# Value products two rows at a time, and a block's own position bias as a factor applied by GpSimd

## What is computed

```python
scores = jnp.einsum('bhid,bhjd->bhij', q, k) / scale
scores = scores + _alibi_bias(N_HEADS, seq_len, M_SLOPE, x.dtype)[None]   # -|i - j| * 0.5 ** head
attn = jax.nn.softmax(scores, axis=-1)
out = jnp.einsum('bhij,bhjd->bhid', attn, v)
```

## Time and profile before

| | |
|---|---|
| median of 3 runs | 598.14 us (596.93 to 600.79) |
| profiled execution, its own time | 600.86 us |
| its span | 598.4 us |
| TensorE busy | 530.7 us, 89% |
| VectorE busy | 406.8 us, 68% |
| ScalarE busy | 339.9 us, 57% |
| GpSimd busy | 217.9 us, 36% |
| mean granted TensorE clock | 0.945 |

### The profile page before, as it was taken

The page is one execution under the profiler, slowest core; times in us unless marked ns, Lnnn a source line. Parts: engine busy times, 40 slices in busy tenths (PEclk is TensorE's granted clock), DMA queues, the critical chain, the costliest instruction groups (busy, mean ns, idle before and its releaser), DMA issues.

```text
span 598.4 us, 11849 instructions
## 1 busy us (share of the span) xinstructions
PE 530.7 (89%) x4499; PEld 298.6 (50%) x4499; DVE 406.8 (68%) x699; ACT 339.9 (57%) x665; POOL 217.9 (36%) x404
## 2 busy tenths in 40 slices
PE   6579999999999999999999999899999389999910
PEld 4234444444445454543445555555656247888710
DVE  2597877878797758789875769988695862232217
ACT  4245766767676767766777667667776013232405
POOL 5736452311234315102640520254012753554540
PEclk9797999999999999999999999999999569999965
DMA  7622343322322222221213333110000114353124
GB/s 162 172 83 76 70 122 87 96 90 77 114 87 73 91 77 100 86 82 48 69 52 70 82 87 104 29 42 21 28 12 19 58 43 109 103 142 81 54 90 133
DMA packets 49991, 48.22 MB, mean 81 GB/s; under 512 B 13923, under 2 KB 39381, under 8 KB 49936
## 3 DMA queue, kind: packets, MB, share of 16 engines
q1 hardware_dynamic: 41600, 32.26, 19.7%
q0 software_dynamic: 5488, 12.73, 6.9%
q10 hardware_dynamic: 2848, 2.49, 1.3%
HBM read 32.00 MB, written 16.06 MB: 80 GB/s over the span
## 4 chain that ended last, share of the span: by engine, by line
PE 72%; DVE 15%; DMA 5%; POOL 3%; issue 2%; ACT 1%; another core or an unknown queue 1%; POOLq 0%; ACTq 0%; DVEq 0%; SPq 0%
PE ps L958 33%; PE ps L1020 17%; DVE row_max L1486 8%; PE ps L1205 6%; PE ps L1219 5%; PE ps L960 4%; POOL xd L845 2%; DMA max_dram<-max_turned 2%; PE ps L1060 1%; DVE x_tok L1796 1%; DMA k_stacks<-k_late 1%; DVE heads L1557 1%; DMA q_stacks<-max_dram 1%; DMA w_nat<-in_qkv_w 1%
## 5 line engine op out<-in xcount | busy, mean ns | idle before, releaser
L1486 DVE TENSOR_REDUCE row_max<-ps 128x1 f32<-128x1024 f32 x256 | 297.1, 1211 | 90.6 <-PE ps L958 47.5
L1323 ACT ACTIVATE probs<-ps 128x512 f32<-128x512 f32 x512 | 268.3, 606 | 89.5 <-PE ps L960 47.8
L958 PE MATMUL ps<-k_stacks,q_stacks 96*128 96x512 bf16 x448 | 145.5, 390 | 13.7 <-DMA k_stacks<-k_late 6.1
L958 PE MATMUL ps<-q_stacks,k_stacks 99*128 99x512 bf16 (+1 forms) x512 | 142.4, 355 | 0.9 <-ACT probs L1323 0.5
L1020 PE MATMUL ps<-probs,v_unit 128*32 128x256 f32 x2048 | 124.0, 382 | 0.0
L960 PE MATMUL ps<-distance,slope_eye 128*128 128x128 bf16 x512 | 110.7, 222 | 0.0
L1020 PEld LDWEIGHTS ps<-probs,v_unit 128*32 128x32 f32 x2048 | 59.9, 109 | 51.4 <-issue 9.4
L958 PEld LDWEIGHTS ps<-k_stacks,q_stacks 96*128 96x128 bf16 x448 | 39.5, 99 | 82.8 <-DVE row_max L1486 27.9
L958 PEld LDWEIGHTS ps<-q_stacks,k_stacks 99*128 99x128 bf16 x512 | 48.7, 98 | 41.6 <-ACT probs L1323 12.2
L960 PEld LDWEIGHTS ps<-distance,slope_eye 128*128 128x128 bf16 x512 | 50.6, 99 | 26.1 <-issue 2.2
L683 POOL TENSOR_TENSOR max_parts<-row_max,no_bits 128x8 bf16<-128x8 f32 x32 | 6.5, 202 | 131.3 <-DVE row_max L1486 129.3
(11 more groups left out here) (264 smaller groups left out, 458.0 us busy)
## 6 DMA issues: line engine op xcount, KB each, us to landing
k_stacks<-k_dram SPq DMA_DIRECT2D x46, 144.0 KB
q_stacks<-q_dram SPq DMA_DIRECT2D x46, 72.0 KB
w<-in_w SPq DMA_DIRECT2D x12, 256.0 KB
xd<-blank POOLq DMA_DIRECT2D x8, 325.0 KB, 2.7
probs<-xd SPq DMA_DIRECT2D x8, 325.0 KB
k_stacks<-in_c_alibi_k SPq DMA_DIRECT2D x24, 96.0 KB
out_dram<-out_t SPq DMA_DIRECT2D x16, 128.0 KB
yt<-zeros POOLq DMA_DIRECT2D x4, 512.0 KB, 3.0
```

The lines of the kernel that those rows point to most:

```text
L958: mm = pe.matmul(out, lhs, rhs, start=True, stop=at is None)
L1323: act.activation(probs[:, k % KEPT, HALF * e:HALF * (e + 1)], ps[:, ring_of(n), :], ACT.Exp).then_inc(ring_read, 1)
L1486: dve.tensor_reduce(row_max[:, m % 2, i:i + 1], max_pair(k).rearrange("p a n -> p (a n)"), AX.X, ALU.max).then_inc(mx_used, 1)
```

## The change

1. `values` takes a pair of rows instead of a half unit. A pair comes after every second row, two pairs behind the exponentials (`BEHIND = 2`): after rows 0 and 1 of unit m come the value products of rows 4 and 5 of unit m - 1, after rows 4 and 5 those of rows 0 and 1 of unit m, and so on. The last two pairs stand behind the loop.
2. The small product leaves the exponentials' side for all heads but the steepest, head 0: 240 of 256 go. Instead `probs` of a block with itself is multiplied by `shade`, a table of exp(-|i - j| * 0.5 ** head). GpSimd does it in place, one operation per row (`shade_own`): 256 elements per partition in a two-head unit, 512 in a four-head unit. In units with own blocks in the first half the four calls stand between `late` of the first half and `copy_v`; in the others behind `late` of the second half and ahead of `split_max`, but row 7's behind `split_max`.
3. The value products of such a row wait for GpSimd's product (`shaded`).
4. `shade` is made at the start: GpSimd sets head 0's part to one, ScalarE takes 15 exponentials of `distance` between `project(3)` and its wait for the first stacks.
5. `shade` takes the place of w1 and w2 in memory, so the first experts' weights (four loads of 256 KB) are loaded by SP when all products with `shade` are done, ahead of `slot_numbers`, and no longer by GpSimd in units 2 and 3.

```diff
+BEHIND = 2
...
-        w1 = [sb(f"w1_{u}", [D, F]) for u in range(2)]
-        w2 = [sb(f"w2_{u}", [P, FT, D]) for u in range(2)]
+        shade = sb("shade", [P, H, P])
+        w1 = [shade[:, 8 * u:8 * u + 4, :].rearrange("p h n -> p (h n)") for u in range(2)]
+        w2 = [shade[:, 8 * u + 4:8 * u + 8, :] for u in range(2)]
...
+            sp.wait_ge(shaded, shaded_by(UNITS - 1, NB - 1))
+            for u in range(2):
+                sp.dma_start(w1[u], t["w1"][u]).then_inc(expert_w_loaded, 16)
+                sp.dma_start(w2[u], t["w2"][u].rearrange("(a p) h -> p a h", p=P)).then_inc(expert_w_loaded, 16)
             sp.dma_start(slot_numbers, t["c_slots"].partition_broadcast(P)).then_inc(numbers_loaded, 16)
...
+            def shade_own(m, j):
+
+                k, n, h = NB * m + j, heads_in(m), head_of(m, 0)
+                at = P * (j - first_block(m))
+                mine = probs[:, k % KEPT, :].rearrange("p (h q) -> p h q", h=n)[:, :, at:at + P]
+                if m == 0 and j == 0:
+                    pool.wait_ge(shade_ready, H)
+                pool.wait_ge(ring_read, reads_by(EXP_PLACE[m, j, 1]) + 1)
+                pool.tensor_tensor(mine, mine, shade[:, h:h + 2 * n - 1:2, :], ALU.mult).then_inc(shaded, 1)
...
-                if m in (2, 3):
-                    u = m - 2
-                    pool.dma_start(w1[u][:], t["w1"][u]).then_inc(expert_w_loaded, 16)
-                    pool.dma_start(w2[u][:], t["w2"][u].rearrange("(a p) h -> p a h", p=P)).then_inc(expert_w_loaded, 16)
...
                 for stage, c in hooks(2 * m):
                     late(stage, c)
+                if own[0] < GROUP:
+                    for j in own:
+                        shade_own(m, j)
...
                 for stage, c in hooks(2 * m + 1):
                     late(stage, c)
+                if own[0] >= GROUP:
+                    for j in own:
+                        if j < NB - 1:
+                            shade_own(m, j)
                 if m + 2 < UNITS:
                     split_max(m + 2)
+                if own[-1] == NB - 1:
+                    shade_own(m, NB - 1)
...
+                    steepest = head_of(m, per * e + i) == 0
                     mm = scores(out[:, n * i:n * (i + 1)], keys(m, per * e + i)[0:K_EXP, P * j:P * (j + 1)],
-                                queries(m, per * e + i)[0:K_EXP], m, per * e + i, at if 0 <= at < n else None)
+                                queries(m, per * e + i)[0:K_EXP], m, per * e + i,
+                                at if own_block(m, j) and steepest else None)
...
-            def values(m, group, half):
-
-                for j in range(GROUP * group, GROUP * (group + 1)):
-                    if j % GROUP == 2:
-                        for stage, c in (hooks(half, (3,)) if half < HALVES else TAIL_FIRST):
+            def values(pair, half, places):
+
+                m = pair // (NB // 2)
+                for j in range(2 * pair % NB, 2 * pair % NB + 2):
+                    if j % 2 == 1:
+                        for stage, c in hooks(half, places):
                             late(stage, c)
                     if j == 0:
                         pe.wait_ge(v_copied, min(m, FOURS + SLOTS - 1) + 1)
                         if m % 2 == 0 and m >= 2:
                             pe.wait_ge(o_kept, m // 2)
                     pe.wait_ge(ring_read, reads_by(EXP_PLACE[m, j, 1]) + 1)
+                    if own_block(m, j):
+                        pe.wait_ge(shaded, shaded_by(m, j))
...
-                    for stage, c in hooks(half, (2,)):
-                        late(stage, c)
-                    if group == 1:
-                        values(m, 0, half)
-                    elif m > 0:
-                        values(m - 1, 1, half)
-            values(UNITS - 1, 1, HALVES)
+                        if j % GROUP == GROUP - 1:
+                            for stage, c in hooks(half, (2,)):
+                                late(stage, c)
+                        pair = (NB * m + j) // 2 - BEHIND
+                        if j % 2 == 1 and pair >= 0:
+                            values(pair, half, (3,) if j % GROUP == GROUP - 1 else ())
+            for pair in range(NB * UNITS // 2 - BEHIND, NB * UNITS // 2):
+                values(pair, HALVES, ())
...
+            act.wait_ge(ld_const, 16 * 3)
+            for h in range(1, H):
+                act.activation(shade[:, h, :], distance[:], ACT.Exp, scale=0.5 ** h).then_inc(shade_ready, 1)
```

16 lines of the change are left out of this document (11 added, 5 removed).

## The result

The kernel after takes 608.14 us (median, 605.03 to 610.2), the kernel before 597.53 beside it: a ratio of 1.0158, 95% interval [1.0112, 1.0205] (it weighs all executions, so it and the later ratios differ by up to 0.3% from the quotient of two medians). It is slower, by some 10 us, and lies outside the range of 590 to 605. Single profiles also differ by up to 2.8 us in the first unit, in how long the clock stays low there, so comparisons of whole times go by the medians, and those of places by differences within a trace.

The account below looks back on a forecast made before the run. TensorE was nearly always busy in the loop, with VectorE pacing rows in halves without own blocks. Gains of 10.4 against losses of 10.9 us made it 0.5 slower than the 598.14 median: 598.6 us, range 590 to 605.

Parts of the forecast that it names:

- six routing halves: Loop halves without own blocks holding long routing work on VectorE: taken as zero change, between -1.5 and +1.5 us.
- Gains, 10.4 us: Sum of savings: 5.7 and 0.4 in own-block halves, 3.1 in the others, 1.2 from moved weight loads.
- 0.26 + 0.12: Predicted gain in us of one quiet half with own blocks and of one quiet half without.
- The DMA wait: TensorE's wait for row maxima at the burst of 93.28, credited 1.2 us for moving the weight loads.
- The copy of `out_t`, 5.5 us: TensorE waiting for ScalarE's copy before an even unit's first value product: 0.39 us lost, fourteen times.
- GpSimd's product late, 4.6 us: Value products of units 11, 14 and 27 waiting for GpSimd: 1.15, 1.15 and 2.3 us lost.
- the 0.8 of the end: Last value product waiting for GpSimd's products of unit 31's last two blocks, behind X2: 0.8 us lost.
- The wait for RANK: TensorE's wait at the head of a routing half, growing from 0.49 to about 1.25 us, twice.
- Contention of GpSimd and VectorE: Slowing of VectorE beside GpSimd: none seen, as four reductions took 4.61 us beside X1 and 4.62 without.
- Rival B: GpSimd's in-place strided product is dearer, 256 elements costing what 512 do: slower, 605 us; chance 0.12.
- Rival D: VectorE paces the loop also in pairs: loop gain falls to 4.4 us, total 604 us; chance 0.04.

Follow-up runs that it names:

- e11: Kernel after with value pairs three behind, RANK two rows later, and small products of units 11, 14 and 31 on TensorE: 593.37 us, ratio 0.9961.
- e4: Kernel before with only the four weight loads moved to SP's queue: 595.9 us, ratio 0.9977.
- e2: Kernel after with value products back in bursts of four rows; GpSimd's factor and moved loads stay: 594.81 us, ratio 0.9962.
- e5: Kernel after with ScalarE's copy of `out_t` moved between the two exponentials of row 4: 602.16 us, ratio 1.0073.
- e7: Kernel after with the small products of units 11, 14 and 27 back on TensorE: 604.21 us, ratio 1.0119.
- e6: Kernel after with TensorE's long waits filled by products nothing reads, or by zeros in unit 27: 603.79 us, ratio 1.0095.
- e14: Kernel before with six unread products ahead of the two row-maximum waits in units 18 and 26: 596.32 us, ratio 0.9974.
- e3: Kernel after with `BEHIND = 3` and the copy of `out_t` after row 5: 600.46 us, ratio 1.005.
- e9: Kernel after with GpSimd's product replaced by a copy of the block onto itself, leaving out the factor: 602.07 us, ratio 1.0113.
- e16: Kernel after with the small products of unit 29 alone on TensorE: 606.73 us, ratio 1.0131.
- e1: Kernel before with only value products by pairs, two behind; small products and weight loads unchanged: 610.05 us, ratio 1.0218.
- e8: Kernel after with bursts of four rows and small products of units 19, 27 and 31 on TensorE: 594.61 us, ratio 0.9941.
- e15: e11 with six unread products ahead of the two row-maximum waits in units 18 and 26: 594.44 us, ratio 0.9954.

## Why the prediction was wrong

The mechanisms that the sum priced were nearly all right. It failed at three steps: it gave the new waits no cost of the clock, it put the six routing halves at zero, and it left out units 30 and 31. Taken by the steps of the sum:

- **Gains, 10.4 us: right in quiet units.** Two bursts of half size and four rows made 5.92 us a half, for 5.90. The lead over the kernel before was 3.8 us at unit 12, and where the pairs are covered (e11) a quiet unit gains 0.33 us, for 0.26 + 0.12. The DMA wait gave 1.06 us (e4; 1.2 in its trace), for 1.2. Also right: alone, the small products give 0.15 us a unit (e2), since VectorE paces the rest.
- **The copy of `out_t`, 5.5 us: right, a little high.** Fourteen waits of 4.8 us together; moving the copy gave back 4.4 us of them in the trace of e5, and 6.0 us of time by the medians with what it did in unit 30 and at the clock.
- **GpSimd's product late, 4.6 us: right, a little high.** The waits stand at the three places, 0.88, 0.45 and 1.98 us for 1.15, 1.15 and 2.3, and one of 0.59 us behind the loop for the 0.8 of the end: 3.9 us in all. e7 gave 3.9 by the medians; its three steps are 4.5, with 1.6 for the clock behind the third in them.
- **The clock behind the waits, not priced: 4.4 us (e6).** Each new wait was priced by its own length, and 1.00 in the earlier trace rows was read as a constant of the loop. The kernel before has waits of 1.1 to 1.5 us in it; its one profile shows no fall behind them, and only e14 shows that there can be one, behind the wait at unit 4. The change adds three places with 1.7 us or more of waiting.
- **The six routing halves, "zero, between -1.5 and +1.5": wrong.** The wait for RANK was forecast at 1.25 us, twice; it measured 1.71 and 1.47, and VectorE's blocks, which were to be borne better by some 0.4 us, did not pay for it: the waits for row maxima behind them are 1.36 and 1.33 us, for 1.32 and 1.47 before. With the clock behind the first RANK, unit 17 alone lost 2.5 us; units 17, 18, 25 and 26 lost 3.3. The text had the mechanism and set a guess against it.
- **Units 30 and 31: left out.** The end was priced at 0.8 us by the last product alone; the trace has 5.5 us before it. 58 of the loop's halves were counted and the last ones not looked at. There VectorE's chain for T1 and ScalarE's exponentials start from a row maximum that comes later in the new rhythm, TensorE waits 1.87 and 1.66 us, for 0.57 before, and 2.6 us more go to the clock (e6). That the second wait is one for the copy of `out_t` is shown by e5, where it shrinks to 1.17 us with the copy one exponential earlier, and by e3 and e11, where it is gone. `turned`, held up by GpSimd's product, is 0.7 us of it (e9, e16).
- **Contention of GpSimd and VectorE, "I see none": wrong reason.** It was argued from reductions, which read PSUM. The operations that it concerns have both inputs in SBUF, and four of them took 1.12, 1.10, 0.97 and 0.43 us for 0.42 and 0.18 to 0.19. Rival B had the name of the mechanism and priced another: GpSimd's product took 0.73 and 1.25 us, for 0.73 and 1.26 forecast, and was not itself the dearer.
- **Rival D's price** is a small slip: gains of 4.4 for 9.2 us make the sum 603.4 us and not 604. It had no weight in the outcome.

In TensorE's waits of this trace: `out_t` 4.8 us, the late products 3.3 in the loop, the RANK waits 2.1 more than before, unit 30 some 3.0 more; and the clock, 5.8 in the trace and 4.4 by the medians. These overlap with the gains and are not a closed sum. e11, which covers nearly all of them, comes 14.8 us under the kernel after. What stays open: what decides whether a given wait is followed by a fall, and how often each place has one, since each kernel has one profile.

The common cause was tested from both sides. The pairs alone lose the most (e1), but about half of that is small products that no longer hide. The changed kernel's pairs one further behind lose little (e3), and with their waits covered they gain (e11); these two change no more than distance and place, but for the small products that e11 gives back to TensorE. The long bursts were not only work; they were the time in which ScalarE, VectorE and GpSimd finished what TensorE needs next. One view misled twice: a loss in one profile was given a cause by its place (GpSimd's lateness in units 18 and 26), where the column of the granted clock held the answer.

## What to carry to other kernels

Before a long block of the busiest engine is split, list every result that was finished under it and ask for each how late it is when the block is half as long; here the cure was distance (one pair further behind) and not less work. Price a new wait of TensorE like those here (1.4 us and up) at its length and, as a risk, as much again for the clock behind it, and look at the granted clock before any other cause is given to a loss; a wait that can't be removed can be filled with products that nothing reads. Look at the last units of a loop by themselves, and when work goes to GpSimd, look for VectorE's operations with two inputs from SBUF and not at its reductions.

## What the runs showed of the hardware

- Waits of TensorE of 1.4 to 2.3 us were followed by stretches at half the granted clock (0.57 in 269:273 and 416:420, 0.50 in 451:457), 1.4 to 2.6 us dear each where a fill took them away. It depends on more than the wait: 1.71 us was followed by such a stretch in the kernel after and by none in e3, e5 and e7; 1.57 in e2, and none behind 1.56 in e8; 1.87 in e15, and none behind 1.88 in e11. Products by zeros, in a wait of 1.39 us, kept the clock up.
- An operation on VectorE with two inputs from SBUF, begun beside a product of GpSimd, ended 0.28 us after it (1.12 us for 0.42). A copy by GpSimd held one in the same way (0.40 us for 0.18, e9). Reductions from PSUM took 1215 ns with and without a product beside them.
- GpSimd's product in place over strided pieces costs what a plain one does, 0.73 us for 256 elements and 1.25 to 1.28 for 512 (the earlier trace rows have 0.73 and 1.26); its copy takes 0.4 and 0.61 us (e9).
